# A two-layer row attention kernel: idle products at the head of a layer, the first k on a second queue, and the third row's q and k one slot sooner

## The chip, the cores and the metric

One NeuronCore of a Trainium2 chip runs the whole kernel. The metric is the device time of one execution in microseconds. Lower is better. The engines named below are TensorE (PE in the profile; PEld is its weight load), VectorE (DVE), ScalarE (ACT), GpSimd (POOL) and SyncE (SP); an engine name with q is the queue of instructions that it issues itself, such as its DMAs.

## What is computed

Two layers of attention with a residual, on x of 128 rows x 256 tokens x 256 channels. Cut to what matters:

```python
# for layer in (0, 1):
n = group_norm(x)                       # 32 groups, mean and variance over all rows, tokens, 8 channels
q, k, v = n @ Wq * 32 ** -0.5, n @ Wk, n @ Wv      # 8 heads of 32 channels
logits = einsum('abhqc,abhkc->abhqk', q, k) + bias (+ mask in layer 1)
w = softmax(logits, axis=-1)            # within one row of 256 tokens
a = einsum('abhqk,abhkc->abhqc', w, v)
x = x + (sigmoid(n @ Wg + gate_bias) * a) @ Wo + bo
```

The normalisation needs the statistics of the whole x. A layer's first row can't be normalised before the last data are in, or before the last row of the layer before is done.

## The kernel before

The rows are worked through one by one in each layer, as a pipeline. A slot s is one turn of every engine's program. `slot(s)` is written out for each engine, and in slot s the engine works on several rows: the projections of row s, the row maxima of row s - 1, the exponentials of rows s - 2 and s - 3, averages, output and residual of older rows. The first ten slots (-2 to 7) and the last four are written out with constants, the others run in loops of four (two on VectorE). The engines order each other by semaphores alone, and each executes its own program in order.

q, k, v and g are products of f16 pieces. x is split in x_hi and x_lo, and a projection (`project`, line 1190) is 12 products of 128x128 weights and 256 columns: six for each half. The fifth product of q waits for x_lo. q and k are split again (`split_high`, `split_f32`, lines 608 and 612; GpSimd's `low_half`, line 549), and the pieces are moved by DMAs of 128 KB into q_stack and k_stack, three each for q and for k. SyncE issues these six per row in the order q_hi (two), k_hi (two), q_lo, k_lo (line 393), behind the two transfers of the shift of row s - 2 (lines 370, 372). The maxima of a row (products line 1201, VectorE line 998) wait for all transfers of its stack. When all eight heads of the row have their maxima, `maxima_rows` transposes them (line 1264) into the first half of proj_b, ScalarE and VectorE turn them into coarse and fine shifts (lines 630 and 1016), and these go into the stack for the exponentials (products line 1206, VectorE line 1010).

TensorE's slot has eight steps. In each stands one head's maxima product of row s - 1 and one head's product for the exponentials. The projections stand between: q at step 1, k at step 2, v at 3 and 4, g at 5. The output stands at 6, the averages of row s - 3 and the transpose of row s - 1 at step 7. In slot 1 both q and k stand ahead of step 0. v and q share the bank proj_a; k, g and the shift share proj_b.

The first row of a layer is prepared by VectorE (`first_row`, lines 974 to 989): x_norm, x_hi, x_lo, then k_hi and k_lo of that row out of proj_b. Before it, `normalisation` forms mean and variance, with two tiny products on TensorE (lines 1448 and 1451) that average over the groups. Around them TensorE runs products of no use, `keep_busy(n, bank)` (line 1176): four before the first average, two before the second, ten after it. In layer 0 they start when the last of 32 statistics loads is used up (`stat_used`), in layer 1 when the last output has left PSUM (`out_left`).

ScalarE's slot also issues the DMAs of x_in (line 684), of the residual and of the result, and writes v_sb (line 702), x_hi (line 721) and the gate (line 728).

## Time and profile before

| | us |
|---|---|
| median of three runs | 3501.84 (3501.17 to 3503.24) |
| profiled execution, device time | 3501.05 |
| its span in the profile | 3499.3 |
| TensorE busy | 3372.0 (96%) |
| VectorE busy | 3345.6 (96%) |
| ScalarE busy | 2909.7 (83%) |
| GpSimd busy | 2984.9 (85%) |
| layer 0's first projection starts | 107.09 |
| layer 1's first idle product starts | 1797.64 |

All times in the views are microseconds from the start of the span. A view by stretches gives the busy time of each engine in the stretch, with the count of its instructions in brackets. The clock column is the share of full speed that was granted to TensorE, where 1.00 is the full level. A timeline row gives start, duration, engine, line of the kernel, instruction, output and inputs, shapes and how many equal ones are merged. Brackets at its end tell how long the engine stood idle before it, and which work ended the wait. Products are pipelined, so the duration of one is longer than the distance to the next.

### The profile page before, as it was taken

What the parts mean: (1) busy time and instruction counts of PE and PEld (TensorE: products, weight loads), DVE (VectorE), ACT (ScalarE), POOL (GpSimd) and SP (SyncE); (2) the same over time, 40 slices, a digit from 0 to 9 for tenths busy, and PEclk for the clock granted to TensorE, in tenths of its full rate; (3) what the DMA queues carried; (4) which work ended last, traced back from release to release, by engine and by line L of the source; (5) the groups of instructions that cost most, each with busy time, mean ns of one, the idle gap of its engine ahead of it and who ended that gap; (6) DMA issues with size and microseconds to landing.
All of it is one profiled execution on the core that took longest, in us unless ns stands there. A gap on an engine that the chain in (4) does not pass through costs nothing. (4 is left out here: it accounts for less than half of the span.)

```text
span 3499.3 us, 122315 instructions
## 1 busy us (share of the span) xinstructions
PE 3372.0 (96%) x36330; PEld 2680.4 (77%) x36330; DVE 3345.6 (96%) x11714; ACT 2909.7 (83%) x5453; POOL 2984.9 (85%) x2055
## 2 busy tenths in 40 slices
PE   0799999999999999999989999999999999999999
PEld 0587778778877877887767877887787788778776
DVE  7899999999999999999979999999999999999999
ACT  3588898889888988988867888888888888888886
POOL 3489889888988898898948988898889889888986
PEclk9999999999999999999999999999999999999999
DMA  9555555555555555555545555555555555555553
GB/s 391 161 125 118 120 126 119 118 124 127 116 119 126 121 118 123 127 117 118 124 141 116 121 120 127 128 119 121 128 122 120 125 128 119 120 128 124 119 124 102
DMA packets 463478, 454.13 MB, mean 130 GB/s; under 512 B 55456, under 2 KB 453920, under 8 KB 462896
## 3 DMA queue, kind: packets, MB, share of 16 engines
q1 hardware_dynamic: 261584, 258.68, 29.9%
q10 hardware_dynamic: 201824, 194.56, 25.8%
q8 instruction: 38, 0.62, 0.1%
q14 instruction: 32, 0.26, 0.0%
HBM read 182.39 MB, written 67.24 MB: 71 GB/s over the span
## 5 line engine op out<-in xcount | busy, mean ns | idle before, releaser
L998 DVE CUSTOM_DVE_ANT_0 max_bank<-max_bank,bias_q 128x256 f32<-128x256 f32 x4096 | 1621.2, 432 | 96.6 <-PE max_bank L1201 96.0
L556 POOL TENSOR_TENSOR probs_sum<-probs 128x1024 f32<-128x1024 f32 x500 | 1186.5, 2373 | 349.3 <-ACT probs L593 168.6
L1010 DVE TENSOR_TENSOR probs<-exp_bank,bias_k 128x512 f32<-128x512 f32 x2048 | 1378.0, 674 | 3.6 <-PE exp_bank L1206 3.6
L1201 PE MATMUL max_bank<-k_stack,q_stack 96*128 96x256 f16 (+1 forms) x4096 | 784.6, 272 | 6.5 <-DVE row_max L998 3.8
L1206 PE MATMUL exp_bank<-q_stack,k_stack 100*128 100x256 f16 x4096 | 780.9, 272 | 2.4 <-DVE probs L1010 2.2
L591 ACT ACTIVATE probs<-probs,mask_bias 128x1024 f32<-128x1024 f32 (+1 forms) x514 | 560.8, 1138 | 37.8 <-issue 29.7
L593 ACT ACTIVATE probs<-probs 128x1024 f32<-128x1024 f32 (+1 forms) x514 | 512.6, 1044 | 44.5 <-issue 25.3
L998 DVE DVE_READ_ACCUMULATOR2_ANT row_max<- 128x1 f32 x4096 | 532.9, 130 | 0.0
L1214 PE MATMUL av_bank<-probs,v_sb 128*32 128x256 f32 x8128 | 492.1, 382 | 0.2
L1201 PEld LDWEIGHTS max_bank<-k_stack,q_stack 96*128 96x128 f16 (+1 forms) x4096 | 401.6, 98 | 55.7 <-DVE row_max L998 6.8
L1206 PEld LDWEIGHTS exp_bank<-q_stack,k_stack 100*128 100x128 f16 x4096 | 393.7, 97 | 64.8 <-DVE probs L1010 7.9
L1214 PEld LDWEIGHTS av_bank<-probs,v_sb 128*32 128x32 f32 x8128 | 237.8, 109 | 184.8 <-issue 53.8
L549 POOL TENSOR_TENSOR q_lo<-q_f,q_hi 128x512 f16<-128x512 f32 x256 | 296.9, 1160 | 95.3 <-ACT q_f L612 95.3
L508 POOL TENSOR_TENSOR gated<-avg,recip 128x512 f32<-128x512 f32 x254 | 325.9, 1283 | 30.3 <-DVE recip L1039 30.3
L630 ACT ACTIVATE coarse<-proj_b 16x128 f16<-16x128 f32 x256 | 68.1, 266 | 339.5 <-PE proj_b L1264 339.5
L523 POOL TENSOR_TENSOR y<-y,attn 128x512 f32<-128x512 f32 x253 | 323.1, 1277 | 2.1 <-ACT attn L664 2.1
L501 POOL TENSOR_TENSOR x_lo<-x_norm,x_hi 128x512 f16<-128x512 f32 x254 | 295.8, 1165 | 14.1 <-ACT x_hi L721 14.1
L516 POOL TENSOR_TENSOR gated_lo<-gated,gated_hi 128x512 f16<-128x512 f32 x254 | 294.8, 1160 | 8.5 <-ACT gated_hi L624 8.5
L549 POOL TENSOR_TENSOR k_lo<-k_f,k_hi 128x512 f16<-128x512 f32 x254 | 295.3, 1163 | 1.7 <-ACT k_f L612 1.6
L696 ACT ACTIVATE x_norm<-x_in,shift_x,rstd 128x256 f32<-128x256 f32 x508 | 274.5, 590 | 0.0
L1221 PE MATMUL den_bank<-probs_sum,head_ones 128*32 128x256 f32 x4000 | 262.2, 379 | 0.2
L664 ACT ACTIVATE attn<-proj_a,out_bias 128x256 f32<-128x256 f32 x502 | 219.5, 468 | 3.6 <-PE proj_a L1272 3.5
(228 smaller groups left out, 6992.9 us busy)
## 6 DMA issues: line engine op xcount, KB each, us to landing
q_stack<-q_hi SPq DMA_DIRECT2D x512, 128.0 KB
k_stack<-k_hi SPq DMA_DIRECT2D x512, 128.0 KB
q_stack<-q_lo SPq DMA_DIRECT2D x256, 128.0 KB
k_stack<-k_lo SPq DMA_DIRECT2D x256, 128.0 KB
x_in<-in_xT ACTq DMA_DIRECT2D x126, 256.0 KB, 3.5
x_in<-layer_out ACTq DMA_DIRECT2D x126, 256.0 KB, 3.6
y<-in_xT ACTq DMA_DIRECT2D x123, 256.0 KB, 3.4
y<-layer_out ACTq DMA_DIRECT2D x123, 256.0 KB, 3.6
```

What stands on the lines that cost most here:

```text
L501: pool.tensor_tensor(x_lo[:, i], x_norm[:, i], x_hi[:, i], ALU.subtract).then_inc(x_lo_ready, 1)
L508: pool.tensor_tensor(gated[:, r.ring(2)].rearrange("p g t -> p (g t)"), avg[:, :, :].rearrange("p g t -> p (g t)"), recip[:, :], ALU.mult) ...
L523: pool.tensor_tensor(y[:, i], y[:, i], attn[:, r.ring(2)], ALU.add).then_inc(y_ready, 1)
L549: pool.tensor_tensor(qk_lo[m][:, b], qk_f32[m][:, b], qk_hi[m][:, b], ALU.subtract).then_inc(qk_lo_ready[m], 1)
L556: pool.tensor_tensor(probs_sum[:, g], pr[:, :, 0, :], pr[:, :, 1, :], ALU.add).then_inc(sum_ready, 1)
L591: act.activation(pr, pr, ACT.Exp, bias=mask_bias[:, bass.ds(r.index(), 1), t]).then_inc(done, 1)
L593: act.activation(pr, pr, ACT.Exp).then_inc(done, 1)
L998: op = dve.tensor_tensor_reduce(out=max_bank[h % 2][:, t, :], in0=max_bank[h % 2][:, t, :], in1=bias_q[:, h, t, :], scale=1.0 / FINE, scal ...
L1010: dve.tensor_tensor(probs[:, r.ring(2), h], exp_bank[h % 2][:, :, :], bias_k[:, h], ALU.add).then_inc(logits_ready, 1)
L1201: op = pe.matmul(bank_[:, t, :], q[0:n, t * P:(t + 1) * P], k[0:n, :], start=True, stop=True)
L1206: op = pe.matmul(bank_[:, t, :], k[0:n, t * P:(t + 1) * P], q[0:n, :], start=True, stop=True)
L1214: op = pe.matmul(bank_[HC * j:HC * (j + 1), g, :], v_sb[:, r.ring(4), t, HC * h:HC * (h + 1)], probs[:, r.ring(2), h, t, :], start=(t == 0 ...
```

## The change

Four things, all in the head of a layer:

- More idle products. In layer 0 twelve start when 31 of the 32 statistics loads are used up. In layer 1 eight stand ahead of the wait for the last output. Before the first average there are six instead of four, before the second six instead of two, and after it fourteen instead of ten.
- The first row's k goes to k_stack by ScalarE's queue: two transfers of k_hi behind x_norm of the next row, and one of k_lo behind v_sb. SyncE leaves these three out.
- Slot 1 has only q ahead of step 0. k stands at step 1. At step 7 of slot 1, ahead of the transpose, q and k of the third row (row 2) are added; they are left out of slot 2, which gets eight idle products at step 7 ahead of its transpose. The transpose of row 0 goes to av_bank instead of proj_b, and k of row 2 doesn't wait for its fine shift.
- On ScalarE, x_hi of row 2 stands ahead of v_sb in slot 1, and q of row 2 is split at the very start of slot 2, ahead of row 0's coarse shift.

```diff
--- before.py
+++ after.py
@@ -78,6 +78,9 @@
 
     def first(self):
         return isinstance(self.turns, int) and self.off == 0
+
+    def is_row(self, n):
+        return isinstance(self.turns, int) and self.off == n
 
     def last(self):
         return isinstance(self.turns, int) and self.off == ROWS - 1
@@ -235,6 +238,10 @@
         pa, pb = bank("proj_a"), bank("proj_b")
         av_bank, den_bank = bank("av_bank"), bank("den_bank")
         shift_ps = pb[0:HEADS * TT, 0, 0:P]
+        first_shift_ps = av_bank[0:HEADS * TT, 0, 0:P]
+
+        def shift_home(r):
+            return first_shift_ps if r.first() else shift_ps
         avg_last = qk_f32[0][:, 0]
         out_last = [pb[:, 0, :], exp_bank[1][:, 1, :]]
 
@@ -387,6 +394,8 @@
                     i, b = s.ring(4), s.ring(2)
                     for m, part, ready, where in ((0, qk_hi, qk_hi_ready, (0, 1)), (1, qk_hi, qk_hi_ready, (0, 2)),
                                                   (0, qk_lo, qk_lo_ready, (2,)), (1, qk_lo, qk_lo_ready, (1,))):
+                        if m == 1 and s.first():
+                            continue
                         wait(sp, ready[m], s.count(1, 1), sp_passed)
                         for w in where:
 
@@ -627,7 +636,7 @@
                 act.wait_ge(shift_psum, r.count(1, 1))
                 q = r.plus(-2)
                 wait(act, shift_in[q.ring(4)], shift_full(q))
-                act.activation(coarse[:, r.ring(2)], shift_ps, ACT.Copy, scale=-FINE / COARSE).then_inc(coarse_ready, 1)
+                act.activation(coarse[:, r.ring(2)], shift_home(r), ACT.Copy, scale=-FINE / COARSE).then_inc(coarse_ready, 1)
 
             def load_residual(r):
                 i = r.ring(4)
@@ -665,14 +674,29 @@
                                         scale=1.0 / (W_SCALE * GATED_SCALE), **kept)
                 op.then_inc(out_left, 1)
 
+            def send_first_k(r, part, ready, where):
+                act.wait_ge(ready, r.count(1, 1))
+                for w in where:
+                    act.dma_start(stack[1][HC * w:HC * (w + 1), r.ring(4)], part[:, r.ring(2)]
+                                  ).then_inc(stack_in[r.ring(4)], 16)
+
+            def high_x(r):
+                i = r.ring(2)
+                act.wait_ge(x_norm_ready, r.count(1, 1))
+                wait(act, g_psum, r.plus(-2).count(1, 1))
+                wait(act, v_psum, r.plus(-2).count(1, 1))
+                act.activation(x_hi[:, i], x_norm[:, i], ACT.Copy).then_inc(x_hi_ready, 1)
+
             def slot(s):
                 l = s.layer
+                if s.is_row(2):
+                    split(s, 0)
                 if s.plus(-2).active():
                     coarse_shift(s.plus(-2))
                 r = s.plus(-3)
                 if r.active():
                     exponentials(r, 0, [0, 1])
-                if s.active():
+                if s.active() and not s.is_row(2):
                     split(s, 0)
                 high_gated(s.plus(-5))
                 if s.active() and not s.first():
@@ -696,6 +720,10 @@
                         op = act.activation(x_norm[:, i, c], x_in[:, i, c], ACT.Identity,
                                             bias=shift_x[:, c:c + 1], scale=rstd[:, c:c + 1])
                     op.then_inc(x_norm_ready, 1)
+                if s.first():
+                    send_first_k(s, qk_hi[1], qk_hi_ready[1], (0, 2))
+                if s.is_row(1):
+                    high_x(s.plus(1))
                 if s.active():
                     act.wait_ge(v_psum, s.count(1, 1))
                     wait(act, av_psum, s.plus(-4).count(2, 2))
@@ -713,12 +741,10 @@
                 if s.plus(-6).active():
                     squares(s.plus(-6))
                 r = s.plus(1)
-                if r.active() and not r.first():
-                    i = r.ring(2)
-                    act.wait_ge(x_norm_ready, r.count(1, 1))
-                    wait(act, g_psum, r.plus(-2).count(1, 1))
-                    wait(act, v_psum, r.plus(-2).count(1, 1))
-                    act.activation(x_hi[:, i], x_norm[:, i], ACT.Copy).then_inc(x_hi_ready, 1)
+                if s.first():
+                    send_first_k(s, qk_lo[1], qk_lo_ready[1], (1,))
+                if r.active() and not r.first() and not s.is_row(1):
+                    high_x(r)
                 if s.active():
                     if s.off == 0 and isinstance(s.turns, int) and l == 0:
                         act.wait_ge(gate_bias_ready, 1)
@@ -1013,7 +1039,7 @@
             def fine_shift(r):
                 i = r.ring(2)
                 dve.wait_ge(coarse_ready, r.count(1, 1))
-                dve.scalar_tensor_tensor(out=fine[:, i], in0=coarse[:, i], scalar=COARSE / FINE, in1=shift_ps,
+                dve.scalar_tensor_tensor(out=fine[:, i], in0=coarse[:, i], scalar=COARSE / FINE, in1=shift_home(r),
                                          op0=ALU.mult, op1=ALU.add).then_inc(fine_ready, 1)
 
             def gated_average(r):
@@ -1261,7 +1287,7 @@
                     pe.wait_ge(gate_ready, r.plus(1).count(1, 1))
                 wait(pe, fine_ready, r.plus(-1).count(1, 1))
                 i = r.ring(2)
-                pe.transpose(shift_ps, row_max[:, i], ident[:, :]).then_inc(shift_psum, 1)
+                pe.transpose(shift_home(r), row_max[:, i], ident[:, :]).then_inc(shift_psum, 1)
 
             def output(r, o, bank_):
 
@@ -1304,16 +1330,16 @@
 
             def project_k(s):
                 wait(pe, gate_ready, s.plus(-1).count(1, 1))
-                wait(pe, fine_ready, s.plus(-2).count(1, 1))
+                if not s.is_row(2):
+                    wait(pe, fine_ready, s.plus(-2).count(1, 1))
                 project(s, 1, pb, 0, None)
                 project(s, 1, pb, 1, k_psum)
 
             def slot(s):
-                second = isinstance(s.turns, int) and s.off == 1
-                if second:
+                early = s.is_row(1) or s.is_row(2)
+                if s.is_row(1):
 
                     project_q(s)
-                    project_k(s)
                 for step in range(8):
                     r = s.plus(-1)
                     if r.active():
@@ -1327,9 +1353,11 @@
                         if h == 0:
                             pe.wait_ge(shift_in[r.ring(4)], shift_full(r))
                         logits(r, h, False)
-                    if step == 1 and s.active() and not second:
+                    if step == 1 and s.active() and not early:
                         project_q(s)
-                    if step == 2 and s.active() and not second:
+                    if step == 2 and s.active() and not early:
+                        project_k(s)
+                    if step == 1 and s.is_row(1):
                         project_k(s)
                     if step == 3 and s.active():
                         pe.wait_ge(qk_f32_ready[0], s.count(1, 1))
@@ -1350,6 +1378,12 @@
                     if step == 7 and r.active():
                         average(r)
                     r = s.plus(-1)
+                    if step == 7 and s.is_row(1):
+
+                        project_q(s.plus(1))
+                        project_k(s.plus(1))
+                    if step == 7 and s.is_row(2):
+                        keep_busy(8, den_bank)
                     if step == 7 and r.active():
                         maxima_rows(r)
 
@@ -1440,16 +1474,19 @@
             for l in range(2):
 
                 if l:
+                    keep_busy(8, den_bank)
                     pe.wait_ge(out_left, ROWS)
                 else:
+                    pe.wait_ge(stat_used, STAT_LOADS - 1)
+                    keep_busy(12, den_bank)
                     pe.wait_ge(stat_used, STAT_LOADS)
-                keep_busy(4, den_bank)
+                keep_busy(6, den_bank)
                 pe.wait_ge(norm_v, 6 * l + 1)
                 pe.matmul(pa[:, 0, 0:CT], group_avg[:, :], mean_var[:, :, 0], start=True, stop=True).then_inc(norm_avg, 1)
-                keep_busy(2, den_bank)
+                keep_busy(6, den_bank)
                 pe.wait_ge(norm_c, l + 1)
                 pe.matmul(pb[:, 0, 0:CT], group_avg[:, :], mean_var[:, :, 1], start=True, stop=True).then_inc(norm_avg, 1)
-                keep_busy(10, den_bank)
+                keep_busy(14, den_bank)
                 slots(pe, l, slot)
                 drain(l)
 
```

## Rows read from the trace of the kernel before

**Rows 1.** The page: busy us, share of the span, instructions.
```profile
PE 3372.0 (96%) x36330; PEld 2680.4 (77%) x36330; DVE 3345.6 (96%) x11714; ACT 2909.7 (83%) x5453; POOL 2984.9 (85%) x2055
```

**Rows 2.** Stretches: us, PE, PEld, DVE, ACT, POOL, clock, DMA, GB/s.
```profile
126.00:136.00 10.00, 7.75 (x70) 6.50 (x68) 8.82 (x37) 5.60 (x12) 3.47 (x3) 1.00 0.57 106
...
136.00:148.00 12.00, 12.00 (x129) 9.04 (x130) 10.88 (x41) 8.51 (x14) 7.72 (x5) 1.00 0.41 89
```

**Rows 3.** Timeline, start of layer 0: start, duration (us), engine, line, instruction.
```profile
94.63 2.40 DVE L836 BATCH_NORM_STATS2 stats<-bias_k 128x6 f32<-128x512 f32 x4
...
104.32 0.59 PE L1451 MATMUL proj_b<-mean_var,group_avg 128*128 128x2 f32 x2 [0.20 <-DVE mean_var L957]
...
104.77 2.29 PE L1176 MATMUL den_bank<-w_hi0q 128*128 128x256 f16 x10
...
106.60 0.43 DVE L980 CAST x_hi<-x_norm 128x512 f16<-128x512 f32 x1
...
107.06 0.69 DVE L982 TENSOR_TENSOR x_lo<-x_norm,x_hi 128x512 f16<-128x512 f32 x1
...
107.09 0.61 PE L1190 MATMUL proj_a<-x_hi,w_hi0q 128*128 128x256 f16 x2
...
109.87 0.43 ACTq L684 DMA_DIRECT2D x_in<-in_xT  x1
...
110.38 0.38 PE L1190 MATMUL proj_b<-x_lo,w_hi0k 128*128 128x256 f16 x2
```

**Rows 4.** Timeline, layer 0, first k to first maxima.
```profile
112.17 1.19 SPq L393 DMA_DIRECT2D k_stack<-k_hi  x2
112.18 0.69 DVE L986 SCALAR_TENSOR_TENSOR k_lo<-proj_b,k_hi 128x512 f16<-128x512 f32 x1
...
114.06 0.60 SPq L393 DMA_DIRECT2D k_stack<-k_lo  x1
...
117.65 0.33 PEld L1201 LDWEIGHTS max_bank<-k_stack,q_stack 96*128 96x128 f16 x4 [0.35 <-DMA k_stack<-k_lo]
```

**Rows 5.** Timeline, start of layer 1.
```profile
1797.64 0.61 PE L1176 MATMUL den_bank<-w_hi0q 128*128 128x256 f16 x4 [1.54 <-ACT attn L767]
...
1800.71 0.59 PE L1451 MATMUL proj_b<-mean_var,group_avg 128*128 128x2 f32 x2 [0.93 <-DVE mean_var L954]
...
1808.62 0.69 DVE L986 SCALAR_TENSOR_TENSOR k_lo<-proj_b,k_hi 128x512 f16<-128x512 f32 x1
...
1811.48 0.60 SPq L393 DMA_DIRECT2D k_stack<-k_lo  x1
...
1814.80 0.33 PEld L1201 LDWEIGHTS max_bank<-k_stack,q_stack 98*128 98x128 f16 x4 [1.03 <-DMA k_stack<-k_lo]
```

**Rows 6.** Stretches of 0.2 us in layer 1, columns as before.
```profile
1799.80:1800.00 0.20, 0.00 (x0) 0.00 (x0) 0.17 (x3) 0.20 (x1) 0.00 (x0) 0.68 0.21 67
1806.60:1806.80 0.20, 0.20 (x3) 0.14 (x2) 0.00 (x0) 0.20 (x1) 0.00 (x0) 0.76 0.00 0
1816.80:1817.00 0.20, 0.00 (x0) 0.00 (x0) 0.20 (x3) 0.00 (x0) 0.00 (x0) 0.84 1.27 359
1820.20:1820.40 0.20, 0.20 (x4) 0.16 (x2) 0.06 (x2) 0.00 (x0) 0.00 (x0) 0.62 0.00 0
```

**Rows 7.** Timeline, both layers: ends of slots 1 and 2.
```profile
123.61 0.43 DVE L998 CUSTOM_DVE_ANT_0 max_bank<-max_bank,bias_q 128x256 f32<-128x256 f32 x1 [0.66 <-PE max_bank L1201]
...
125.30 0.28 PE L1264 MATMUL proj_b<-ident,row_max 128*16 128x128 f32 x1 [1.51 <-DVE row_max L998]
...
135.10 0.28 PE L1264 MATMUL proj_b<-ident,row_max 128*16 128x128 f32 x1 [1.63 <-DVE row_max L998]
...
136.00 0.39 PE L1201 MATMUL max_bank<-k_stack,q_stack 96*128 96x256 f16 x2 [0.62 <-DMA k_stack<-k_lo]
...
1824.04 0.28 PE L1264 MATMUL proj_b<-ident,row_max 128*16 128x128 f32 x1 [1.51 <-DVE row_max L998]
...
1835.28 0.39 PE L1201 MATMUL max_bank<-k_stack,q_stack 98*128 98x256 f16 x2 [1.17 <-DMA k_stack<-k_lo]
```


## The prediction

> **What bounds the kernel now.** I read the page's busy shares first. TensorE is busy 3372.0 us, 96% of the span, VectorE 3345.6, also 96% [rows 1]. Then I asked for stretches. Once the pipeline of rows is full, between 136 and 148 us, TensorE is busy in 12.00 of 12.00 us [rows 2]: each later slot starts when TensorE has finished the one before, so a slot that begins x us sooner ends the layer x us sooner. Before that TensorE isn't full: from 126 to 136 us it is busy 7.75 us of 10 while VectorE has 8.82 [rows 2]. So the question is at what time slot 3 starts in either layer: 136.00 and 1835.28 us [rows 7]. The third view was the timeline of the two heads, from the statistics to that point. The reader is to see in it two spacings of the same product: a pair takes 0.61 us and ten take 2.29 us at the head, thus (2.29 - 0.61) / 8 = 0.21 us each, and a pair takes 0.38 and four take 0.61 later, thus 0.11 each [rows 3, 5]. For 256 columns these are the levels 1.2 and 2.4 GHz. The clock column shows it for layer 1: it falls near 1799.9, rises near 1806.7, falls again near 1816.9 and rises near 1820.3 [rows 6]. In layer 0 the column starts only with the first change, so the spacing is the witness there: slow until about 110.1, fast by 110.38 [rows 3].
>
> **The change, part by part.** Times are those of the profiled execution (3501.05 us, span 3499.3); the median of the runs is 3501.84, 0.8 more, and I add that at the end.
>
> 1. **Products at the head of layer 0.** Twelve start after the 31st statistics load, which ends at 94.63 + 2.40 = 97.03 [rows 3]; at 0.21 they end at 99.6, while VectorE works on: free by themselves. Six instead of four before the first average end at 102.8, before it is due. Six instead of two before the second average cost something if the clock is low: the average now begins at 104.32 and would begin about 104.8, so x_hi, which ends at 107.03, comes 0.5 later. Fourteen instead of ten then run from 105.3 to 108.3 at 0.21 each, so the first q projection would begin at 108.3, not 107.09 [rows 3]. Two ends follow. Slow case, the clock rises at 110.1 as now: q and k have 24 products, 8 of them slow by then and 16 fast, and the first k_lo begins 0.6 later than 112.18 [rows 4]. Fast case, the denser work lifts the clock about 106.7: the filler ends 107.5, q starts 107.6, waits for x_lo at 108.3, and k_lo begins 0.6 sooner. No row says which; I take the middle, 0, and keep +-0.6.
>
> 2. **Products at the head of layer 1.** Eight now follow the last output product, six instead of four lie before the first average, six instead of two before the second. The clock fell near 1799.9 [rows 6] after a stretch that held only those four, the average and two more [rows 5]. It now holds about three times as many. I take it that the clock stays up: the second average (0.59 us slow, 0.38 at the level of the pairs) gives 0.2, and 13 of the 24 products of q and k that ran at 0.21 run at 0.11, 1.3. So k_lo begins 1.5 sooner than 1808.62 [rows 5]. If it falls all the same, 14 slow products push q, and k_lo begins 0.4 later.
>
> 3. **First k on ScalarE's queue.** Now k_lo's transfer waits on SyncE behind two of k_hi and one of q_lo: it is issued 1.88 us after k_lo starts in layer 0 (112.18 to 114.06) and 2.86 after in layer 1 (1808.62 to 1811.48) [rows 4, 5]. On ScalarE it stands behind two k_hi issues only. An issue costs 0.43 there for another shape [rows 3] and 0.60 on SyncE [rows 4]; two make 0.9 to 1.2, and k_lo's own data take 0.69. So about 1.2 after, a gain of 0.7 and 1.65. What is queued behind the three issues on ScalarE: v_sb, x_hi of the second row, the gate. x_hi leads to x_lo on GpSimd and so to the second row's q, which stands ahead of the first maxima. In layer 0 that has slack, in layer 1 with the gain of step 2 it is about level; its price is 0 to 0.8, I take 0.4 in layer 1.
>
> The Trainium skill, DMA: Bandwidth & Descriptors, "Issuing engines are not separate DMA queues", says that DMAs of all engines run on the same 16 DMA engines and that a second issuer saves only issue time. By it this step gives its issue time at best; rival C is what that would be here where the engines are full.
>
> 4. **Row 0's maxima to slot 3.** Now 117.65 to 136.00 = 18.35 us, and 1814.80 to 1835.28 = 20.48 [rows 4, 5, 7]. Layer 1's is longer through the slow stretch from 1816.9 to 1820.3 [rows 6], some 14 products more at 0.10 each, and a longer wait for the third row's transfer, 1.17 against 0.62 [rows 7]. After the change slot 1 carries q and k of the third row too: the last maxima product is issued some 5.85 us in (the second row's g still holds VectorE for 0.66, rows 7), 24 products at 0.11 follow, and the transpose comes at 8.5 instead of 7.65 (117.65 to 125.30) [rows 4, 7]. They need x_lo of row 2, which ScalarE now allows before v_sb, about 5.9 in. VectorE idles about a microsecond there. Slot 2 loses these 24 products but is VectorE's: 9.80 now (125.30 to 135.10) [rows 7], of which 8.8 to 9.0 are work [rows 2]; about 9.4 remain, and 0.1 to slot 3. The eight products of slot 2's end (0.9) lie under TensorE's wait of 1.63 for VectorE [rows 7]. The third row's transfers are issued behind the two shift transfers of row 0, some 4 us before they are needed, so the waits of 0.62 and 1.17 [rows 7] go. Sum 8.5 + 9.4 + 0.1 = 18.0. Gain 0.35 and 2.5. Row 0's shift in av_bank costs nothing: that bank's first average is a slot later.
>
> **Sum.** Layer 0: 0 + 0.7 + 0.35 = 1.05 gained, 0.45 to 1.65. Layer 1: 1.5 + 1.65 - 0.4 + 2.5 = 5.25; I count 5.0, since x_lo of row 2 and the landing leave no slack. Together 6.0: 3501.05 - 6.0 = 3495.05, and with 0.8 for the median 3495.8.
>
> **Rivals.** A, the clock falls at layer 1's head all the same: step 2 is -0.4 instead of 1.5, the 0.4 of step 3 goes, so 1.5 less, 3497.3; for it speaks that the waits for the averages stay as long as they were [rows 5]. B, all goes well: the fast case in layer 0 and nothing lost on ScalarE: 1.65 + 5.65 = 7.3, 3494.5. C, the transfers land no sooner for being issued sooner, because they share the engines with the second x_in: the 0.7 and 1.65 of step 3 are gone, 3.65 in all, 3498.2; against it, DMA is only 0.41 to 0.57 busy in the stretches seen [rows 2]. D, slower: the fillers lie in TensorE's order ahead of the averages and of q, and the third row's q and k ahead of row 0's transpose. If the clock is low in both heads (+0.6, +0.4), if ScalarE's issues eat the queue's gain, and if slot 2 doesn't shrink (+0.85 a layer), the sum is +2.7: 3504.5. It decides from the point where VectorE needs its whole 9.8 us in slot 2; its 8.82 busy of 10 [rows 2] speaks against. E, nothing comes of it: the slots re-align on a later wait, 3501.8; the full TensorE of 136 to 148 us speaks against.
>
> The Trainium skill, TensorE: Matmul & The Clock Gate, "What's actually happening", says that throttled is the default and activity releases it, and that the point of release varies from run to run. No run here shows that variation; it is a reason why one profile's rise at 110.1 need not be the median's.
>
> **How the numbers follow.** Forecast 0.45, A 0.18, B 0.14, C 0.10, D 0.08, E 0.05. 0.2% is 7.0 us, about what a measurement can tell from no change. B and 0.12 of the forecast's spread go beyond it, so faster 0.26, slower 0.02, same 0.72. The range leaves out D, E and a little below: 3492.5 to 3501.0.
>
> **What would show it.** Clock column at 1 from 1799 to 1822; x_hi of layer 0 later than 107.03 by 0.5; k_lo's issue on ScalarE's queue near 1.2 after k_lo; the first maxima near 117.65 - 0.7 = 116.9 and, measured from layer 1's first product at 1797.64 [rows 5], 14.4 us on instead of 17.2; the transposes of row 0 8.5 us after them; slot 3 without a DMA wait, near 135.0 in layer 0. I am wrong if slot 2 stays at 9.8, or if the clock record still shows the fall near 1799.9.

## The result and the profile after

| | before | changed |
|---|---|---|
| median of 15 runs, us | 3503.21 (3500.49 to 3507.53) | 3496.19 (3494.99 to 3497.80) |
| ratio | | 0.9981 (0.9974 to 0.9988) |
| profiled execution, device time | 3501.05 | 3497.80 |
| its span | 3499.3 | 3495.9 |

The changed kernel takes 7.0 us less, 0.19% (0.12 to 0.26%). Two things stand beside the gain. The kernel before spreads over 7 us, the changed one over 3. And the profiled execution of before was one of its fastest, that of the changed kernel its slowest, so the two profiles differ by 3.3 us only (3501.05 to 3497.80).

The page, as in [rows 1]: busy us, share of the span, instructions. TensorE has 56 products more and is 5 us longer busy. The time is not in the busy shares.

```profile
PE 3377.2 (97%) x36386; PEld 2682.9 (77%) x36386; DVE 3345.2 (96%) x11714; ACT 2909.8 (83%) x5453; POOL 2986.4 (85%) x2055
```

The timeline of the changed kernel, head of layer 0, answers [rows 3, 4] (columns: start, duration, engine, line, instruction, what ended the idle time).

```profile
97.17 2.72 PE L1202 MATMUL den_bank<-w_hi0q 128*128 128x256 f16 x12 [97.17 <-DVE stats L862]
...
104.75 0.43 PE L1488 MATMUL proj_b<-mean_var,group_avg 128*128 128x2 f32 x2
...
106.87 0.43 DVE L1006 CAST x_hi<-x_norm 128x512 f16<-128x512 f32 x1
...
107.98 0.63 PE L1216 MATMUL proj_a<-x_hi,w_hi0q 128*128 128x256 f16 x2
...
112.30 1.33 ACTq L680 DMA_DIRECT2D k_stack<-k_hi  x2
112.30 0.69 DVE L1012 SCALAR_TENSOR_TENSOR k_lo<-proj_b,k_hi 128x512 f16<-128x512 f32 x1
...
113.70 0.59 ACTq L680 DMA_DIRECT2D k_stack<-k_lo  x1
...
117.23 0.33 PEld L1227 LDWEIGHTS max_bank<-k_stack,q_stack 96*128 96x128 f16 x4 [0.15 <-DMA k_stack<-k_lo]
```

The second average starts 0.43 later than in [rows 3], x_hi 0.27 later (106.60 to 106.87), q's first product 0.89 later (107.09 to 107.98). By k_lo only 0.12 of this is left (112.18 to 112.30). The first maxima come 0.42 sooner than in [rows 4], 4.94 after k_lo's start instead of 5.48.

The same timeline at the head of layer 1 answers [rows 5].

```profile
1797.51 1.04 PE L1202 MATMUL den_bank<-w_hi0q 128*128 128x256 f16 x8
1799.22 0.83 PE L1202 MATMUL den_bank<-w_hi0q 128*128 128x256 f16 x6 [0.67 <-ACT attn L793]
...
1802.30 0.38 PE L1488 MATMUL proj_b<-mean_var,group_avg 128*128 128x2 f32 x2 [0.49 <-DVE mean_var L980]
...
1808.71 0.69 DVE L1012 SCALAR_TENSOR_TENSOR k_lo<-proj_b,k_hi 128x512 f16<-128x512 f32 x1
...
1810.11 0.56 ACTq L680 DMA_DIRECT2D k_stack<-k_lo  x1
...
1813.71 0.61 PE L1227 MATMUL max_bank<-k_stack,q_stack 98*128 98x256 f16 x4
```

Six idle products take 0.83 us, the second average 0.38: all at the higher level. From the first idle product behind the wait for the last output, k_lo starts 9.49 us on instead of 10.98, and the first maxima 14.49 instead of 17.17.

The stretches of [rows 6] again, and two of layer 0 (columns: stretch, sum, busy PE, PEld, DVE, ACT, POOL with counts, granted clock, DMA share, GB/s).

```profile
1799.80:1800.00 0.20, 0.20 (x3) 0.00 (x0) 0.13 (x1) 0.20 (x2) 0.00 (x0) 1.00 0.94 338
...
1816.80:1817.00 0.20, 0.20 (x4) 0.18 (x3) 0.20 (x3) 0.20 (x1) 0.17 (x1) 1.00 1.05 164
...
136.80:137.00 0.20, 0.20 (x4) 0.14 (x2) 0.20 (x3) 0.20 (x1) 0.00 (x0) 0.67 0.01 1
137.00:137.20 0.20, 0.20 (x3) 0.13 (x2) 0.20 (x3) 0.20 (x1) 0.00 (x0) 0.50 0.00 0
```

Both falls of layer 1 are gone. A new one stands in layer 0 from 136.9 to about 140.2, behind the start of slot 3. What it costs is measured below, by a second profile of the same kernel.

The timeline at the ends of slots 1 and 2 answers [rows 7].

```profile
125.83 0.27 PE L1290 MATMUL av_bank<-ident,row_max 128*16 128x128 f32 x1
...
134.82 0.28 PE L1290 MATMUL proj_b<-ident,row_max 128*16 128x128 f32 x1 [0.75 <-DVE row_max L1024]
...
136.03 0.39 PE L1227 MATMUL max_bank<-k_stack,q_stack 96*128 96x256 f16 x2 [0.93 <-DMA k_stack<-k_lo]
...
1822.30 0.27 PE L1290 MATMUL av_bank<-ident,row_max 128*16 128x128 f32 x1
...
1831.36 0.28 PE L1290 MATMUL proj_b<-ident,row_max 128*16 128x128 f32 x1 [0.75 <-DVE row_max L1024]
...
1832.08 0.39 PE L1227 MATMUL max_bank<-k_stack,q_stack 98*128 98x256 f16 x2 [0.44 <-DMA k_stack<-k_lo]
```

Slot 1 takes 8.59 us to its transpose in both layers, slot 2 takes 8.99 and 9.06. But slot 3 still waits for the third row's k_lo, 0.93 and 0.44. SyncE's instructions of layer 0 show why.

```profile
127.60 0.54 SPq L379 DMA_DIRECT2D q_stack<-fine  x1
128.18 1.67 SPq L402 DMA_DIRECT2D q_stack<-q_hi  x2
129.90 1.39 SPq L402 DMA_DIRECT2D k_stack<-k_hi  x2
131.33 1.60 SPq L402 DMA_DIRECT2D q_stack<-q_lo  x1
132.98 0.60 SPq L402 DMA_DIRECT2D k_stack<-k_lo  x1
```

The six transfers are queued behind fine. Single issues take from 0.54 to 1.60 us, and k_lo goes out at 132.98, later than in the kernel before (131.41). That is 1.84 ahead of slot 3's start (134.82), and the wait ends 3.05 after it.

### The profile page after: what moved, and what is told of

It is laid out like the page before. It is cut to its first block and busy times, and to the rows that moved or that the text cites. A ratio compares the mean times of both kernels' runs of the same rounds, so it can differ in the third digit from the quotient of the medians.

```text
span 3495.9 us, 122425 instructions
## 1 busy us (share of the span) xinstructions
PE 3377.2 (97%) x36386; PEld 2682.9 (77%) x36386; DVE 3345.2 (96%) x11714; ACT 2909.8 (83%) x5453; POOL 2986.4 (85%) x2055
```

## The experiments

Every kernel was also timed, in 11 runs each (12 for head products in layer 1 only, of which one, at 12490.8, stands out and is left out of its median; 8 for the second look at before). The medians of before beside them were 3502.11, 3503.06 and 3501.80 in the three groups of runs, so a difference between groups is uncertain by about 1 us; inside a group it is better. Group 1 ran on another chip than groups 2 and 3, and the changed kernel itself ran in group 1 only. In group 2 the nearest to it is head products in layer 1 only (3495.88), in group 3 eight products more in slot 2 (3496.45). In the table, "third transpose" is the start of row 2's transpose in layer 0. "Layer 1" is the time from the first idle product behind the wait for the last output to row 2's transpose there. Both are from the profiled execution. Between the two all kernels run alike: from the transpose in layer 0 to that idle product it is 1649.4 to 1650.3 us in all of them. "Falls" are the times at which the clock column goes below 1, behind its first rise.

| kernel | group | median us | third transpose | layer 1 | falls |
|---|---|---|---|---|---|
| before (first profile) | | 3503.21 | 147.92 | 49.74 | 1800, 1817 |
| before again | 3 | 3502.12 | 148.36 | 47.65 | 135, 1801 |
| changed (first profile) | | 3496.19 | 149.61 | 44.96 | 137 |
| changed again | 1 | 3495.59 | 147.53 | 45.33 | none |
| head products alone | 1 | 3499.23 | 149.97 | 45.55 | 136 |
| no head products | 1 | 3499.41 | 146.92 | 49.04 | 1799, 1812 |
| first k on SyncE | 1 | 3496.12 | 148.04 | 44.76 | none |
| third row back | 2 | 3499.64 | 149.50 | 46.15 | 137 |
| head products in layer 1 only | 2 | 3495.88 | 147.15 | 44.87 | none |
| third k on ScalarE too | 2 | 3496.63 | 147.81 | 45.14 | none |
| x_in behind k_lo | 2 | 3497.83 | 147.52 | 46.18 | 104 |
| no products in slot 2 | 3 | 3499.78 | 149.41 | 46.58 | 136, 1833 |
| third row back, slot 2's products kept | 3 | 3497.70 | 148.52 | 46.03 | none |
| eight products more in slot 2 | 3 | 3496.45 | 147.59 | 45.14 | none |

### Both kernels again

> The changed kernel again, beside the others of this group. Theory 1 (the gain is in the heads, nearly all in layer 1): 6 to 7 us under the kernel before in the median, the start of slot 3 about 4.8 us sooner after layer 1's first idle product, and no gain in layer 0, where the third row's k_lo lands late. Theory 2 (most of the difference of the medians is falls of the clock that come and go between executions): the difference of the medians falls below 4 us, and the trace shows the clock falls at other places than before.

Measured: 3495.59 (3494.97 to 3496.29), ratio 0.9981 (0.9972 to 0.9990). This profile has no fall at all. The third transpose is 2.08 sooner than in the first profile of the same kernel. Of this 0.42 stood before slot 3 (136.03 to 135.61); the fall from 136.9 to 140.2 is the other 1.66, slot 3 taking 13.58 us with it and 11.92 without.

> The kernel before once more, for a second profile of it. If its median lies above its first profile because the clock falls at more places in most executions, this profile shows a fall near 136 us in layer 0 that the first did not have, or two in layer 1; slots of the loop stay at 13.02 us each. Rival: the slots of the loop themselves are longer.

Measured: 3502.12 (3499.69 to 3507.68). The profile is one of 3499.69. It has a fall in layer 0, from 135 to 139, that the first one lacked, and it lacks the fall at 1816.9. So the falls of the kernel before stand at other places in these two executions, and a single profile shows one draw. Neither is a typical one. Each timed run has its mean granted clock on record, and both profiled executions have 0.999. Of the 101 runs of before in the three groups 33 have 0.999 (median 3500.62), 50 have 0.998 (3502.54) and 18 have 0.997 (3506.09), where the changed kernel has 1.000 in 10 of 11. Most executions of before thus hold more time at the lower level than either profile; at which places, no profile shows.

### The products at the heads

Edit: no head products, the rest as in the changed kernel.

```diff
-                    keep_busy(8, den_bank)
                     pe.wait_ge(out_left, ROWS)
                 else:
-                    pe.wait_ge(stat_used, STAT_LOADS - 1)
-                    keep_busy(12, den_bank)
...
-                keep_busy(6, den_bank)
+                keep_busy(4, den_bank)
...
-                keep_busy(6, den_bank)
+                keep_busy(2, den_bank)
...
-                keep_busy(14, den_bank)
+                keep_busy(10, den_bank)
```

> The changed kernel with the idle products at the heads as they were (4, 2, 10, none ahead of the wait in layer 1); the eight in slot 2 stay. Theory 1: the clock falls at layer 1's head again and the changed kernel loses 1.5 to 3 us, so 3.5 to 5 us under the kernel before. Theory 2: the median moves less than 1 us from the changed kernel's.

Measured: 3499.41, 3.8 more than the changed kernel in the same group. Stretches of its trace in layer 1:

```profile
1798.80:1799.00 0.20, 0.00 (x0) 0.00 (x0) 0.17 (x3) 0.20 (x1) 0.00 (x0) 0.59 0.14 49
1805.60:1805.80 0.20, 0.20 (x4) 0.15 (x2) 0.00 (x0) 0.20 (x1) 0.00 (x0) 0.84 0.00 0
1812.60:1812.80 0.20, 0.00 (x0) 0.00 (x0) 0.00 (x0) 0.00 (x0) 0.20 (x1) 0.50 0.08 10
```

The fall comes at 1798.8 to 1798.9, some 2.3 us after the first idle product (1796.56), about as long after it as in [rows 5, 6] (1797.64 to 1799.9). A second one follows. Layer 1 takes 49.04 instead of 45.33.

Edit: layer 0 has its old numbers back, layer 1 keeps its own.

```diff
-                    pe.wait_ge(stat_used, STAT_LOADS - 1)
-                    keep_busy(12, den_bank)
                     pe.wait_ge(stat_used, STAT_LOADS)
-                keep_busy(6, den_bank)
+                keep_busy(6 if l else 4, den_bank)
...
-                keep_busy(6, den_bank)
+                keep_busy(6 if l else 2, den_bank)
...
-                keep_busy(14, den_bank)
+                keep_busy(14 if l else 10, den_bank)
```

> The changed kernel with layer 0's idle products as they were (4, 2, 10) and layer 1's as changed. Theory 1: layer 0 neither wins nor loses by them (x_hi 0.25 sooner, the clock's rise later): within 0.7 us of the changed kernel, and all of the 3.8 us that the products are worth is layer 1's. Rival: layer 0's products are worth 1 us or more, and this is slower by that.

Measured: 3495.88, 0.3 more than the changed kernel's 3495.59, which is inside the groups' uncertainty. Its x_hi starts at 106.78, against 106.87 and 106.95 in the two profiles of the changed kernel. Layer 0's products are worth nothing that can be measured; the 3.8 is layer 1's.

Edit: the head products put into the kernel before, and nothing else.

```diff
+                    keep_busy(8, den_bank)
                     pe.wait_ge(out_left, ROWS)
                 else:
+                    pe.wait_ge(stat_used, STAT_LOADS - 1)
+                    keep_busy(12, den_bank)
...
-                keep_busy(4, den_bank)
+                keep_busy(6, den_bank)
...
-                keep_busy(2, den_bank)
+                keep_busy(6, den_bank)
...
-                keep_busy(10, den_bank)
+                keep_busy(14, den_bank)
```

> The kernel before with only the idle products at both heads changed (12, 6, 6, 14 and 8). Theory 1: layer 1's first k_lo starts 1.2 to 1.5 us sooner after the first idle product, the clock holds there, and the late stretch after the first maxima may still fall; layer 0's x_hi comes 0.27 later and nothing is won there. Together 1.5 to 3 us faster. Theory 2: within 1 us of the kernel before.

Measured: 3499.23, 2.9 less than before. The rest of the change alone (no head products) gives 2.7. Together they give 6.5. The 0.9 that this is more than the sum is within what medians of 11 runs can tell. The head of layer 1 kept its clock in all 11 profiles of kernels with these products, and lost it within some 3 us in all 3 without them.

### The first k's queue

Edit: the first k on SyncE, the rest as in the changed kernel.

```diff
-                        if m == 1 and s.first():
-                            continue
...
-                if s.first():
-                    send_first_k(s, qk_hi[1], qk_hi_ready[1], (0, 2))
...
-                if s.first():
-                    send_first_k(s, qk_lo[1], qk_lo_ready[1], (1,))
```

> The changed kernel with the first row's k again issued by SyncE. Theory 1: the first maxima come 0.7 us later in layer 0 and 1 to 1.6 later in layer 1, since k_lo waits behind k_hi and q_lo; 1.5 to 2.3 us slower than the changed kernel. Rival (the landing is set by the 16 DMA engines, not by the issue): less than 0.5 us slower.

Measured: 3496.12, 0.5 more than the changed kernel. In layer 0 its first maxima come at 117.88 instead of 116.93, 5.87 after k_lo's start instead of 4.98. In layer 1 there is no loss. The changed kernel (second profile) there, then this one; in the view of DMA each digit is the busy share, in tenths, of a fortieth of the time from 1805 to 1815 us.

```profile
1808.37 0.55 ACTq L680 DMA_DIRECT2D k_stack<-k_lo  x1
...
1812.62 0.61 PE L1227 MATMUL max_bank<-k_stack,q_stack 98*128 98x256 f16 x4 [0.52 <-DMA k_stack<-k_lo]
```
```profile
DMA  0000486997999999999999999420000000009549
```
```profile
1809.09 0.60 SPq L400 DMA_DIRECT2D k_stack<-k_lo  x1
...
1812.17 0.61 PE L1221 MATMUL max_bank<-k_stack,q_stack 98*128 98x256 f16 x4 [0.77 <-DMA k_stack<-k_lo]
```
```profile
DMA  3000048887899496896988992200000007729500
```

Measured from k_lo's start (1806.96 and 1807.09), on ScalarE its transfer is issued 0.59 sooner (1.41 instead of 2.00) and the wait ends 0.58 later (5.66 instead of 5.08): 4.25 us after issue instead of 3.08. This profile is the latest of its kind. In the first profile of the changed kernel and in four others with the same order and the clock up (head products in layer 1 only, third k on ScalarE too, no products in slot 2, eight more) the first maxima come 4.97 to 5.26 after k_lo's start, neither sooner nor later than on SyncE. The DMA engines are at 9 tenths or more from 1807.5 to 1811.25 in the changed kernel, and mostly at 6 to 9 from 1806.5 to 1811 in the other. With the engines that full, the transfer issued sooner didn't land sooner. The Trainium skill, DMA: Bandwidth & Descriptors, "Issuing engines are not separate DMA queues", says that the DMAs of all issuing engines run on the same 16 DMA engines and interleave, and that a second issuer saves only the time of issuing. The trace of layer 1 agrees: the gain is not more than the 0.59 of earlier issue, and in fact nothing. In layer 0 it differs: the gain is 0.89 and the issue 0.54 sooner.

Edit: in the first slot ScalarE issues the x_in load behind k_lo instead of ahead of x_norm.

```diff
-                r = s.plus(2)
-                if r.active() and s.active():
+                def load_x(r):
...
+                if s.plus(2).active() and s.active() and not s.first():
+                    load_x(s.plus(2))
...
                     send_first_k(s, qk_lo[1], qk_lo_ready[1], (1,))
+                    load_x(s.plus(2))
```

> The changed kernel with the transfer of row 2's x (256 KB) issued behind the first row's k_lo instead of ahead of its k_hi. If full DMA engines set the landing of the first k_lo, it lands 0.5 to 1 us sooner after its issue in layer 1 and the first maxima follow; 0.5 to 1 us faster. If the issue sets it, no change.

Measured: 3497.83, 2.0 more than its group's 3495.88, which neither case of the expectation had. In layer 1 k_lo is issued at 1807.95 and x_in at 1808.56, behind it, where it was 1805.14.

```profile
1807.95 0.57 ACTq L680 DMA_DIRECT2D k_stack<-k_lo  x1
1808.56 0.62 ACTq L707 DMA_DIRECT2D x_in<-layer_out  x1
...
1813.06 0.61 PE L1230 MATMUL max_bank<-k_stack,q_stack 98*128 98x256 f16 x4 [0.69 <-DMA k_stack<-k_lo]
```

The wait now ends 5.11 us after the issue. So it isn't x_in's place ahead of k_lo that delays it: with 256 KB behind it, it comes later still. In which order the engines serve two queues stays open. The fall at 104 in this profile lies ahead of the edit's place: the six idle products at 101.59 ran in 0.83 us, the higher level, where all other profiles still had the lower one there.

Edit: the third row's k goes by ScalarE's queue too.

```diff
-                        if m == 1 and s.first():
+                        if m == 1 and (s.first() or s.is_row(2)):
                             continue
...
+                if s.is_row(2):
+                    send_first_k(s, qk_hi[1], qk_hi_ready[1], (0, 2))
...
+                if s.is_row(2):
+                    send_first_k(s, qk_lo[1], qk_lo_ready[1], (1,))
```

> The changed kernel with the third row's k (k_hi, k_hi, k_lo) also issued by ScalarE. If the remaining wait for that k_lo (0.9 us in layer 0, 0.4 in layer 1) comes from SyncE's order, it goes and the kernel is 1 to 1.3 us faster. If the 16 DMA engines set it, k_lo lands as late and nothing changes.

Measured: 3496.63, no gain (its group has 3495.88). Slot 3 doesn't wait for k_lo any more. Another wait has come, in slot 2:

```profile
128.73 0.55 ACTq L680 DMA_DIRECT2D k_stack<-k_lo  x1
...
130.45 0.39 PE L1236 MATMUL exp_bank<-q_stack,k_stack 100*128 100x256 f16 x2 [0.68 <-DMA q_stack<-fine]
```

The third row's k_hi now goes out at 127.02 and 127.64 on ScalarE, beside the fine shift on SyncE (127.69), and slot 2 has to wait for the fine shift. Slot 2 takes 9.83 (125.94 to 135.77) instead of 8.91 (125.53 to 134.44), and slot 3 12.04 (to 147.81) instead of 13.09. So SyncE's order was what held k_lo back: on ScalarE it goes out at 128.73 instead of 132.57, and its wait is gone. But the 1.05 that slot 3 gains is lost again in slot 2 but for 0.13.

### The third row and slot 2's products

Edit: the changed kernel without slot 2's idle products.

```diff
-                    if step == 7 and s.is_row(2):
-                        keep_busy(8, den_bank)
```

> The changed kernel without the eight idle products at the end of slot 2. They lie under TensorE's wait for VectorE, so they cost nothing; if they keep the clock up, their absence lets it fall near 136 us in some executions and the median rises by 0.5 to 2 us and the spread widens. Rival: they do nothing, and the median stays within 0.3 us.

Measured: 3499.78, 4.2 more than the changed kernel and 3.3 more than the version with sixteen such products in the same group. The timeline of this kernel, and its stretches of one us:

```profile
134.90 0.28 PE L1290 MATMUL proj_b<-ident,row_max 128*16 128x128 f32 x1 [1.63 <-DVE row_max L1024]
135.84 0.39 PE L1227 MATMUL max_bank<-k_stack,q_stack 96*128 96x256 f16 x2 [0.66 <-DMA k_stack<-k_lo]
```
```profile
134.00:135.00 1.00, 0.10 (x1) 0.09 (x1) 1.00 (x6) 0.00 (x0) 0.00 (x0) 1.00 0.47 132
135.00:136.00 1.00, 0.34 (x3) 0.16 (x3) 0.39 (x1) 0.78 (x2) 0.00 (x0) 1.00 0.00 0
136.00:137.00 1.00, 1.00 (x8) 0.78 (x7) 0.73 (x5) 1.00 (x2) 0.00 (x0) 0.70 0.03 4
137.00:138.00 1.00, 1.00 (x7) 0.73 (x5) 1.00 (x5) 0.43 (x1) 0.49 (x1) 0.50 0.00 0
```

The changed kernel, second profile, the same stretches:

```profile
134.00:135.00 1.00, 0.28 (x1) 0.09 (x1) 0.93 (x4) 0.24 (x2) 0.00 (x0) 1.00 0.31 85
135.00:136.00 1.00, 0.39 (x4) 0.35 (x5) 0.00 (x0) 1.00 (x3) 0.00 (x0) 1.00 0.00 0
136.00:137.00 1.00, 1.00 (x12) 0.88 (x10) 0.95 (x6) 0.96 (x2) 0.00 (x0) 1.00 0.03 4
137.00:138.00 1.00, 1.00 (x11) 0.90 (x10) 1.00 (x5) 0.00 (x0) 0.96 (x1) 1.00 0.00 0
```

Without the products TensorE stands idle for 1.63 and again for 0.66 us. The clock falls as slot 3 begins, and slot 3 runs 7 products a microsecond instead of 11. TensorE is full there, so this time isn't hidden: from row 1's transpose to row 2's it is 14.51 us (134.90 to 149.41) instead of 13.09. It happens in layer 1 too (1831.07 to 1845.53, 14.46, instead of 12.78). The two stages lose 1.88 and 1.25 (third transpose and layer 1 in the table), 3.1 of the 3.5 between the two profiles. The timed runs agree: all 11 have a mean granted clock of 0.999, where 10 of 11 have 1.000 with sixteen products. Over all profiles, layer 0 has this fall in 4 of 5 without the products and in 1 of 9 with them. In layer 1 it is 1 of 5 and none of 9, although TensorE's first gap is 1.63 there too. Why the same gap seldom leads to a fall there isn't shown.

Edit: q and k of the third row, its x_hi and its split (ScalarE) stand where they stood before, row 0's shift is in proj_b again, and slot 2's products are out. With them k of the second row stands ahead of step 0 of slot 1 again.

```diff
-                early = s.is_row(1) or s.is_row(2)
+                early = s.is_row(1)
                 if s.is_row(1):

                     project_q(s)
+                    project_k(s)
...
-                        project_k(s)
-                    if step == 1 and s.is_row(1):
                         project_k(s)
...
-                    if step == 7 and s.is_row(1):
-
-                        project_q(s.plus(1))
-                        project_k(s.plus(1))
-                    if step == 7 and s.is_row(2):
-                        keep_busy(8, den_bank)
```

> The changed kernel with the third row's q and k again in slot 2, the second row's k ahead of step 0 of slot 1, the first shift in proj_b and no products in slot 2. Products at the heads and the first k on ScalarE stay. Theory 1: slot 1 shrinks from 8.6 to about 7.6 us, slot 2 grows from 9.0 to 9.8 and the wait for the third row's k_lo is 0.8 to 1.2, so about 1 us slower in layer 0 and 1 in layer 1, 1.5 to 2.5 in all. Rival: the later transpose of row 0 eats what slot 2 gives, and it is within 0.7 us of the changed kernel.

Measured: 3499.64, 3.8 more than the best of its group (head products in layer 1 only). Slots 1 and 2 of layer 0 take 7.64 and 9.80, as expected; that the median loses more than the expected 1.5 to 2.5 goes with the fall at 137.

Edit: as the last, but these two lines stay.

```diff
                     if step == 7 and s.is_row(2):
                         keep_busy(8, den_bank)
```

> The changed kernel with the third row's q and k back in slot 2, but the eight idle products of slot 2 kept. If the order itself is what the 4 us of the third row's move are, this stays near 3499.6. If the eight products are, it comes to 3496 to 3497.

Measured: 3497.70, and no falls. So the products alone recover 1.9 in the median. What is left to the changed order is 1.3 inside the group (3496.45), 2.1 across groups, and 1.0 + 0.7 in the two stages of the table (148.52 to 147.53, 46.03 to 45.33).

It isn't the order of the third row. The first maxima of this kernel:

```profile
118.34 0.60 PE L1223 MATMUL max_bank<-k_stack,q_stack 96*128 96x256 f16 x4
...
1813.84 0.60 PE L1223 MATMUL max_bank<-k_stack,q_stack 98*128 98x256 f16 x4
```

From here to row 2's transpose it takes 30.18 and 30.27 us. The changed kernel's second profile takes 30.60 and 30.18 (116.93 to 147.53, 1812.62 to 1842.80). So the move of the third row's q and k gains nothing in either layer. The loss stands ahead of the first maxima, where this edit has put k of the second row back. They start this long after k_lo's start (layer 0, layer 1; one profile each, all with the head products):

| first row's k by | second row's k ahead of step 0 | second row's k at step 1 |
|---|---|---|
| SyncE | 5.93, 5.48 (head products alone) | 5.87, 5.08 (first k on SyncE) |
| ScalarE | 6.20, 6.28 (this kernel) | 4.98, 5.66 (changed, second profile) |

The first profile of the changed kernel has 4.94 and 5.00. ScalarE's queue alone loses 0.27 and 0.80, since x_hi of the second row stands behind its issues. The later k alone gains 0.06 and 0.40. Both together gain 0.95 to 0.99 in layer 0 and -0.18 to 0.48 in layer 1.

Edit: the changed kernel with eight products more, behind slot 2's transpose.

```diff
                         maxima_rows(r)
+                    if step == 7 and s.is_row(2):
+                        keep_busy(8, den_bank)
```

> The changed kernel with eight more idle products behind the transpose of slot 2, in the wait of 0.9 us for the third row's k_lo. If falls of the clock at 136 us still cost the changed kernel something, it is 0.3 to 1 us faster in the median; if the wait in layer 1 (0.4 us) is shorter than the products, it loses 0.4 there. Rival: no difference.

Measured: 3496.45, not less than the changed kernel (3495.59 in group 1). No version tried is faster than the changed kernel by more than these runs can tell.

## Why the prediction came out as it did

Predicted 3495.8, measured 3496.2. The total is right; of its parts two are right, two are wrong in size or in reason, and one mechanism that carries 3 to 4 us was priced at nothing. That the total agrees is in part luck. It starts from 3501.84, the median of three runs of before; the median of fifteen is 3503.21. The gain was forecast at 6.0 and measured at 7.0, and inside it terms that were lost and a term that was left out make up for each other.

**1. Layer 0's products: right.** Nothing was forecast, with 0.5 for x_hi. Measured: x_hi 0.27 to 0.35 later, k_lo 0.12 later or 0.23 sooner than in before's first profile, 0.3 in the median. Before's second profile has x_hi at 106.83 and k_lo already at 111.16, so k_lo moves by a microsecond between executions of one kernel, about the whole width of the forecast's +-0.6. Neither of the two cases named came out clean: q started 0.9 late, as in the slow case, and caught up.

**2. Layer 1's products: right.** k_lo was to come 1.5 sooner and came 1.49 sooner, by the mechanism named, and taking the products away brings the fall back. Rival A is out. They bring more than the step counted, 3.8 in the median, and in two of the three profiles without them a second fall follows in layer 1's first slots, at 1816.9 in [rows 6] and at 1812.5 in the experiment. The prediction put that second fall under step 4.

**3. First k on ScalarE: mis-sized.** The issue came 1.4 after k_lo's start, 1.2 was forecast. The sum had 0.7 + 1.65 - 0.4 = 1.95 for it; taking it away costs 0.5. Two readings failed. The 2.86 us of [rows 5] were taken for the queue's order, but with the clock up SyncE has k_lo out 2.0 after its start (1807.09 to 1809.09), so part had gone already. The difference is the pair of k_hi issues: 2.17, 2.70 and 2.58 us in the three profiles in which the clock fell at layer 1's head, 1.25 to 1.29 in the eleven others; what makes them longer isn't shown. And the 0.41 to 0.57 of DMA in [rows 2] that spoke against rival C are means over 10 and 12 us further on; the stretch that matters, 1807.5 to 1811.25, is nearly full. Rival C is right for layer 1 and wrong for layer 0. The price on x_lo of the second row is real (it starts 2.88 after k_lo's start instead of 2.06). It is hidden only because the change also takes k of the second row out of the way, which the prediction gave no price: with that k ahead of step 0 the queue costs 0.27 and 0.80.

**4. Slots 1 and 2: the sum nearly right in layer 1, for the wrong reason in part.** Slot 1 was forecast at 8.5 and took 8.59. Slot 2 was forecast at 9.4 and took 9.0. But 0.1 was forecast to slot 3, and it took 1.21 and 0.72: the waits for k_lo didn't go. "Some 4 us before they are needed" was 1.84 in layer 0 and 3.36 in layer 1 (1828.00 to 1831.36), since they go out behind fine and single issues took up to 1.60. So layer 0 has 18.79 us (117.24 to 136.03) where 18.0 was forecast and 18.35 stood before. In layer 1 it is 18.37 instead of 20.48, 2.1 gained where 2.5 was forecast; yet before's second profile, without the fall at 1816.9, has 18.95 there. Most of the 2.1 is the clock. Set against the kernel with slot 2's products and the old order, the third row's move brings -0.42 and 0.09 from the first maxima to row 2's transpose: what slot 2 gives, slot 1 and the wait take.

The larger miss is a sentence of this step: the eight products of slot 2 "lie under TensorE's wait of 1.63". They do, and nothing was put down for them. Taking them away costs 3.3 to 4.2. The row that pointed there was [rows 7]: waits of 1.63 and then 0.62 or 1.17 in a row, just ahead of a stretch where TensorE is full [rows 2]. The first profile of before showed no fall behind them, and the prediction read that one profile as the rule, against its own sentence that the point of release varies from run to run, which no trace had shown then. The traces show it now: the kernel before falls at 1800 and 1817 in one execution and at 135 and 1801 in another.

**The sum.** 6.0 was forecast from profile to profile. The profiles give 3.3 (first) and 4.8 (3501.05 to 3496.29, second), of it 4.8 and 4.4 in layer 1, where 5.0 was forecast, and -1.7 and +0.4 in layer 0, where 1.05 was forecast. The 0.8 added for the median supposed that both kernels lie as far from their profile. Before lies 2.2 above its own (3503.21 to 3501.05), the changed kernel at -1.6 and -0.7. Against before's second profile (3499.69) the gain is only 1.9 and 3.4. So the terms lost in steps 3 and 4 are about made up by falls that the changed kernel seldom has; that is argued from the medians, not counted. How often the kernel before has the one near 136 isn't known: one of its two profiles shows it, and all three of other kernels without slot 2's products. That it has more low time than its two profiles show is on record (a mean clock of 0.998 or less in 68 of 101 runs). Rival B is out, since layer 0's fast case didn't come; so are D and E, since the changed kernel is faster than before in both comparisons.

## What to carry to other kernels

Price a gap of an engine that is off the bound by what follows it: TensorE idle for 1.6 + 0.7 us just ahead of a full stretch was followed by a fall in 4 of 5 profiles in layer 0 and in 1 of 5 in layer 1, at 1.4 us or more each, and idle products in the gap, free by the wait, gave it back. Read the DMA share of the very microseconds in which a transfer must land before counting on an earlier issue. Where a change moves two things at once, try each alone: here a queue that cost 0.3 to 0.8 us by itself paid only beside a reordering that the prediction had not priced. Where executions spread by 7 us and the clock record falls at different places, take a second profile before reading one as typical.

## What the runs showed of the hardware that was not expected

- The issue of one 128 KB transfer is not of constant length: 0.60 us for most, 1.60 for q_lo at 131.33 in the changed kernel. A pair of k_hi took 2.17 at 1808.61 in the kernel before, and 1.25 with the first k on SyncE.
- With two queues in place of one the last transfer took longer from its issue to the end of the wait: 4.25 us instead of 3.08 in layer 1, at DMA engines that were fuller (3.56 to 3.87 and 3.47 in other profiles of either kind). With 256 KB queued behind it, 5.11.
- The clock fell in layer 0 behind two short gaps (1.63 and 0.58 to 0.89 us) with little work between them, in 4 of 5 profiles, and in the changed kernel's first profile behind 0.75 and 0.93. In layer 1 it fell behind such gaps (1.63 and 0.41) in 1 of 5. The low level lasts 3 to 4 us there even though TensorE is full from the first of them on.
